# Logic attention: values ahead of the last gates and the projection between turning and right product, with four smaller edits

## The reference, cut to what matters

```
h = concat(tokens(x), txt)
h += logic_attention(ln(h))      # 8 heads: S1 = q1 k1', S2 = q2 k2', A1, A2 = softmax(S1), softmax(S2)
                                 # feat = S1, S2, S1', S2', log(A1 A2 + eps), log(A2 A1 + eps)
                                 # hid = gelu(conv1 feat), gates = sigmoid(conv2 hid)
                                 # A = softmax(mix of S1, S2, log(A1 A2) by the gates)
                                 # y = (A v1 + w A1 (A2 v2)) proj_w
h += expert_choice(ln(h))        # 8 experts take their top 28 of 113 tokens of an image, gelu MLP 128-256-128
h += relative_attention(ln(h))   # 8 heads, relative positions for keys and values
h += lstm_experts(ln(h))         # top 2 of 8 experts a token; each expert is an LSTM over the 32 images
                                 # out = h_t Wo + bo, weighted
```

## Time and profile before

| | us |
|---|---|
| median of 3 runs (2335.65 to 2337.36) | 2337.19 |
| the profiled execution's own time | 2334.96 |
| its span | 2333.2 |
| TensorE busy | 2127.5 (91%) |
| VectorE busy | 1746.5 (75%) |
| ScalarE busy | 1670.2 (72%) |
| GpSimd busy | 360.5 (15%) |
| GELU, L792, 480 of them | 451.0 |
| LSTM gates, L1871 and L1879 | 467.4 and 447.5 |
| convolution, L606 | 305.3 |

### The profile page before, as it was taken

How to read it: one execution, slowest core, us unless ns; L and a number is a source line. 1 busy time by engine, 2 the same in 40 slices (tenths; PEclk the granted TensorE clock), 3 DMA queues, 4 the chain that set the end, 5 groups by cost and what they waited for, 6 DMA issues and landing times. The chain is left out here.

```text
span 2333.2 us, 55453 instructions
## 1 busy us (share of the span) xinstructions
PE 2127.5 (91%) x22214; PEld 1521.6 (65%) x22214; DVE 1746.5 (75%) x2674; ACT 1670.2 (72%) x3076; POOL 360.5 (15%) x198
## 2 busy tenths in 40 slices
PE   6589999999999999998649799987899999999998
PEld 3454455554455554453237588856799999999997
DVE  4348999999999999998644344535788888888886
ACT  3468898888888888888723336732777777777776
POOL 0222322333322333222000013410000000000000
PEclk9589999999999999999759868998899999999999
DMA  6188888888888888888210000001222222212220
GB/s 184 57 235 236 224 228 238 233 241 239 227 224 237 232 237 239 229 228 217 61 46 1 10 2 2 1 25 74 84 77 70 72 67 77 77 61 73 71 77 21
DMA packets 113208, 305.19 MB, mean 131 GB/s; under 512 B 20495, under 2 KB 57481, under 8 KB 112442
## 3 DMA queue, kind: packets, MB, share of 16 engines
q1 hardware_dynamic: 112954, 301.66, 45.8%
HBM read 168.64 MB, written 80.65 MB: 107 GB/s over the span
## 5 line engine op out<-in xcount | busy, mean ns | idle before, releaser
L792 ACT ACTIVATE la_hid<-ps,la_b 128x904 f32<-128x904 f32 (+1 forms) x480 | 451.0, 991 | 57.3 <-PE ps L606 56.6
L1871 PE MATMUL ps<-ls_xm,ls_w_in_parts 128*128 128x226 f16 x3072 | 467.4, 261 | 4.9 <-ACT ls_cells L1921 4.3
L1879 PE MATMUL ps<-ls_state_parts,ls_w_rec_parts 128*128 128x226 f16 x2976 | 447.5, 259 | 0.0
L1921 ACT ACTIVATE ls_gates<-ps,ls_bias 128x226 f32<-128x226 f32 x768 | 301.2, 446 | 120.9 <-PE ps L1879 120.1
L606 PE MATMUL ps<-la_pairs,la_w 32*64 32x452 f32 x3584 | 305.3, 568 | 5.1 <-ACT la_hid L792 4.9
L1871 PEld LDWEIGHTS ps<-ls_xm,ls_w_in_parts 128*128 128x128 f16 x3072 | 294.2, 97 | 14.6 <-issue 3.6
L1879 PEld LDWEIGHTS ps<-ls_state_parts,ls_w_rec_parts 128*128 128x128 f16 x2976 | 284.9, 96 | 6.0
L621 PE MATMUL ps<-la_hid,la_w 128*32 128x452 f32 x1856 | 240.9, 556 | 22.4 <-ACT la_opened L798 22.4
L567 POOL TENSOR_TENSOR weights_or_rows<-la_S,la_top 113x904 f32<-113x904 f32 x64 | 133.3, 2084 | 554.3 <-DVE la_top L939 554.3
L621 PEld LDWEIGHTS ps<-la_hid,la_w 128*32 128x32 f32 x1856 | 42.3, 108 | 202.1 <-issue 94.1
L2006 DVE TENSOR_TENSOR ls_state<-ls_gates,ls_tc 128x452 f32<-128x452 f32 x128 | 80.5, 629 | 109.5 <-ACT ls_tc L1928 109.2
(11 more groups left out here) (294 smaller groups left out, 4132.1 us busy)
## 6 DMA issues: line engine op xcount, KB each, us to landing
la_pairs<-la_maps SPq DMA_DIRECT2D x224, 452.0 KB, 6.2
la_gate<-la_opened SPq DMA_DIRECT2D x448, 113.0 KB, 4.0
...
```

Of the source, the lines that this page charges most:

```text
L792: act.activation(hid[:, u % 4, 0:n], ps[:, bank:bank + n, 0:HALF], ACT.Gelu_apprx_tanh, bias=b1[:])\
L1871: mm = pe.matmul(out_j, w_in_parts[:, w, e, j, :], xm[:, t % 2, e, :, x, 0:N], start=((w, x) == PASSES[0]), stop=(t == 0 and (w, x) == PAS ...
L1879: mm = pe.matmul(out_j, w_rec_parts[:, w, e, j, :], state_parts[:, x, e], start=False, stop=((w, x) == PASSES[-1]))
L1921: return act.activation(dst, ps[:, n % 3 * 2 + j // 2, j % 2 * 256:j % 2 * 256 + C], ACT.Tanh if j == 3 else ACT.Sigmoid, bias=bias[:, e, ...
```

## The change

Five edits.

1. Logic attention, each period. TensorE runs `values(f)` before gates 7 rather than behind the turning, and `project(p + 4)` between turning and right product rather than behind `base`. VectorE copies the values first, and the projection's results directly behind the turned softmaxes. `turn_mix` waits for this period's keys (`qk_ready`).
2. Its start. The scores of images 0 to 2 go to four pairs of banks; GpSimd scales before it shifts, VectorE sums before it copies.
3. Its end. The order of the eight row groups becomes `TURNS`, groups 2 and 3 are gated and group 6 is turned earlier, the square root's table is loaded ahead, and VectorE scales the last four images.
4. Expert choice. The memset of `hid` goes to GpSimd, the wait for weights behind the gathers, and the choice of the second half of the images behind the first half's gathers.
5. LSTM experts. The bias product takes f16 in three stacked parts (48 rows: high, low, high against high, high, low), one pass; the weights are stored as two f16 parts as well.

```diff
@@ -477,9 +477,14 @@
-        def scored():
-
-            return ps[0:N, X:X + 2, 0:HALF].rearrange("p k (s m) -> p k s m", s=4)
+        def bank_of(z, i):
+
+            return (X, CB, CA, GA)[i] if z < 3 else X
+
+        def scored(z, i):
+
+            bank = bank_of(z, i)
+            return ps[0:N, bank:bank + 2, 0:HALF].rearrange("p k (s m) -> p k s m", s=4)
@@ -570,13 +575,15 @@
                     m, c, f, z = p - 1, p, p + 2, p + 3
-                    if ok(z):
+                    if ok(z) and p >= 0:
                         shift(z, 0)
...
                             pool.tensor_tensor(x, x, per_head(inv[:, i * H:(i + 1) * H]), ALU.mult).then_inc(s["P_ready"], 1)
+                    if ok(z) and p < 0:
+                        shift(z, 0)
                     if ok(z):
@@ -630,6 +637,10 @@
                             after(pe, s["added"], z - 5)
+                            after(pe, s["ST_out"], 2 * z)
+                        elif z < 3:
+                            if i == 3:
+                                after(pe, s["ych_ready"], z - 1)
                         elif i < 3:
@@ -641,19 +652,23 @@
                             sides = k[rows, col(t)], q[rows, i % 2, col(t)]
-                            mm = pe.matmul(ps[0:N, X + bank, col(2 * t + part)], *(sides if i < 2 else sides[::-1]),
+                            mm = pe.matmul(ps[0:N, bank_of(z, i) + bank, col(2 * t + part)], *(sides if i < 2 else sides[::-1]),
                                            start=True, stop=True)
...
                     after(pe, s["ln_ready"], 2 * f)
+                    if f < 2:
+                        pe.wait_ge(s["ST_out"] if i == 0 else s["S_out"], 2 * f + (4 if i == 0 else 3))
                     for hd in range(H):
...
                     pe.wait_ge(s["S_out"], 2 * min(f + 2, B))
+                    if f < 2:
+                        pe.wait_ge(s["ST_out"], 2 * f + 4)
                     pe.matmul(ps[0:N, X, 0:2 * D], hT[:, f, :], w_v[:], start=True, stop=True).then_inc(s["V_made"], 1)
@@ -679,7 +694,7 @@
                     after(pe, s["opened_ready"], PAIRS * min(e + 3, B))
-                    after(pe, s["qk_ready"], min(e + 6, B))
+                    after(pe, s["qk_ready"], min(e + 7, B))
                     after(pe, s["ych_ready"], min(e + 4, B))
@@ -705,7 +720,9 @@
                 def project(b):
-                    after(pe, s["ET_ready"], b - 5)
+                    if 0 < b < 4:
+                        pe.wait_ge(s["S_out"], 2 * b)
+                    after(pe, s["ET_ready"], b - 6)
                     after(pe, s["opened_ready"], PAIRS * min(b - 3, B))
@@ -718,7 +735,7 @@
-                    pe.wait_ge(s["rows_ready"], k + 1)
+                    pe.wait_ge(s["rows_ready"], TURNS.index(k) + 1)
                     if k == 0:
@@ -751,12 +768,16 @@
                                 score(p + 3, i, part)
+                    if ok(f):
+                        values(f)
                     if ok(p):
...
                         turn_softmax(f, 1)
-                        values(f)
+                    if ok(p + 4):
+                        project(p + 4)
+                    if ok(f):
                         right_product(f)
@@ -765,18 +786,22 @@
                                 gate_rows(four - 2)
+                        gate_rows(2)
+                        gate_rows(3)
+                    if p == B + 1:
+                        turn_rows(6)
                     if ok(f):
...
                         base(e)
-                    if ok(p + 4):
-                        project(p + 4)
                     if ok(e):
                         output(e)
-                for four in range(4, 8):
-                    turn_rows(four)
-                    gate_rows(four - 2)
+                turn_rows(4)
+                turn_rows(5)
                 gate_rows(6)
+                gate_rows(4)
+                turn_rows(7)
+                gate_rows(5)
                 gate_rows(7)
@@ -895,12 +920,13 @@
                         root(0, slice(0, EARLY))
-                for k in range(4, 7):
+                for k in (6, 4, 5):
                     scale_rows(k)
-                for k in range(4, 7):
-                    move_rows(k)
+                move_rows(6)
+                act.preload_act_table_set("sqrt_and_others")
+                move_rows(4)
                 root(1, slice(EARLY, B))
-                scale_rows(7)
+                move_rows(5)
                 move_rows(7)
@@ -1076,13 +1102,15 @@
                         mix_sum(m)
+                    if ok(f) and p < 0:
+                        sums(f)
                     if ok(z):
...
                         top_of(z, 0)
-                    if ok(f):
+                    if ok(f) and p >= 0:
                         sums(f)
@@ -1095,8 +1123,10 @@
                     if ok(f):
+                        values(f)
                         turned_softmax(f)
-                        values(f)
+                    if ok(p + 4):
+                        projected(p + 4)
                     if ok(m):
@@ -1105,13 +1135,15 @@
                         attended(e)
-                    if ok(p + 4):
-                        projected(p + 4)
                     if ok(e):
...
                 row_scale(1, slice(EARLY, B))
+                dve.wait_ge(s["row_scale"], 2)
+                for b in range(EARLY, B):
+                    x = dve.tensor_scalar(rows[:, b, :], h[:, b, :], ln["rstd"][:, b:b + 1], ln["offset"][:, b:b + 1], ALU.mult, ALU.add)
+                x.then_inc(s["rows_ready"], 1)
@@ -1207,23 +1239,26 @@
-                pe.wait_ge(consts_in, 80)
                 pe.wait_ge(s["gate_ready"], 1)
...
                 tr.then_inc(s["rows_made"], 1)
-                for k in range(2):
+                def turn_back(k):
                     pe.wait_ge(s["chosen"], k + 1)
                     pe.transpose(ps[0:N, 6 + k, 0:128], rank[:, k, :], ident[:]).then_inc(s["turned_back"], 1)
-                pe.wait_ge(s["place_ready"], 2)
+
+                turn_back(0)
                 for q in range(GROUPS):
...
                     turn(q)
+                pe.wait_ge(consts_in, 80)
                 for n in range(2 * E):
...
                         second(n - 1)
+                    if n == 1:
+                        turn_back(1)
                     if n % 2 and n < E:
@@ -1257,6 +1292,10 @@
                         take_chosen(GROUPS + n // 2)
+
+            @block.gpsimd
+            def _(pool):
+                pool.memset(hid[:], 0.0).then_inc(s["hid_zero"], 1)
@@ -1291,7 +1330,6 @@
                 steps.done(dve.memset(ones[:], 1.0))
-                dve.memset(hid[:], 0.0).then_inc(s["hid_zero"], 1)
                 scores, by_bank = scores_of(ps), peak[:].rearrange("p (k i) -> p k i", i=4)
@@ -1319,14 +1357,23 @@
                     dve.tensor_tensor(rank[:, k, :], rank[:, k, :], above[:, k, :], ALU.mult).then_inc(s["chosen"], 1)
-                for k in range(2):
+
+                def places(k):
                     dve.wait_ge(s["turned_back"], k + 1)
...
                                                 ps[0:N, 6 + k, 0:128].rearrange("p (b e) -> p b e", e=E)), s["place_ready"], k + 1)
+
+                choose(0)
+                places(0)
+                dve.wait_ge(consts_in, 80)
                 one_hot(0)
                 for q in range(GROUPS):
-                    one_hot(q + 1)
+                    if q + 1 < GROUPS:
+                        one_hot(q + 1)
                     take_back(q)
+                choose(1)
+                places(1)
+                one_hot(GROUPS)
                 for n in range(E):
@@ -1709,6 +1756,7 @@
     w_dram = nc.dram_tensor("ls_weights", (T * E * K, N), F32, kind="Internal").ap()
+    parts_dram = nc.dram_tensor("ls_weight_parts", (2, T * E * K, N), F16, kind="Internal").ap()
     halves = (slice(0, N - 1), slice(N - 1, N))
@@ -1776,6 +1828,9 @@
                     sp.dma_start(w_dram[rows, :].rearrange("(k p) n -> p k n", p=128), turned_w[:, ks, :]).then_inc(s["w_stored"], 16)
+                    for i in range(2):
+                        sp.dma_start(parts_dram[i, rows, :].rearrange("(k p) n -> p k n", p=128), turned_w_parts[:, i, ks, :])\
+                          .then_inc(s["w_stored"], 16)
@@ -1789,13 +1844,14 @@
                     rows = slice(t * E * K, (t + 1) * E * K)
-                    sp.wait_ge(s["w_stored"], 16 if t < FIRST else 32)
+                    sp.wait_ge(s["w_stored"], 48 if t < FIRST else 96)
                     if t >= 2:
...
                                  w_dram[rows, :].rearrange("r n -> (r n)").partition_broadcast(D)).then_inc(weights_in[k], 16)
-                    sp.dma_start(w_row[:, k], w_dram[rows, :]).then_inc(weights_in[k], 16)
+                    for i in range(3):
+                        sp.dma_start(w_row[E * K * i:E * K * (i + 1), k], parts_dram[i % 2, rows, :]).then_inc(weights_in[k], 16)
@@ -1826,7 +1882,7 @@
```

(26 more changed lines are left out.)

35 lines of the change are left out of this document (20 added, 15 removed).

## The result

The changed kernel takes 2346.22 us, the median of 6 runs (2340.94 to 2349.82); before takes 2337.28 in as many. The ratio is 1.0037 with a 95% interval of 1.002 to 1.0054: a little slower, with the whole interval above 1. A second set of 10 runs on another occasion gave 2341.28 and 1.002 (1.0007 to 1.0034). The forecast was 2332, inside a range up to 2342.

What follows compares the result with a forecast made beforehand. ScalarE was taken to pace part of logic attention, with no slack at L1012/L834, and TensorE the LSTM phase. Terms +22.6 - 11.7 - 6.5 - 7.1 - 7.9 + 6.0 = -4.6 gave 2332 us, range 2325 to 2339.

Steps and rivals of the forecast that it cites:

- 1. The steady period: Logic attention's repeated period: moving values and projection earlier costs +0.80 us a period, +22.6 in all (12.9 to 33).
- both routes: Steady period: delays through TensorE and through VectorE each give +0.80 us, run side by side and do not add.
- rival E: Steady period: the mix's turning waits for the projection's key copy, +1.2 us a period, 2343 us; chance 0.08.
- 2. The start: Logic attention's start: four bank pairs and scaling before shifting bring the first convolution from 143.75 to 132.0, -11.7 us.
- 3. The end: Logic attention's end: closing TensorE's idle gap and moving gate passes and one turning earlier gives -6.5 us.
- 4. Expert choice: Expert choice: memset moved, weight wait removed and half the choice deferred give -7.1 us net.
- 5. The bias product: LSTM experts: one f16 pass for two f32 passes saves 0.255 us a step, -7.9 over 31 steps.
- 6. The LSTM's start: LSTM experts' start: the masks' load, queued behind stores waiting for VectorE, comes late, +6.0 us (+3 to +6.8).
- A: Steady period: it does not grow, as filled holes on TensorE might pay; 2310 us, chance 0.12.
- B: Steady period: only the values' 0.43 us counts, +12.9 instead of +22.6; 2323 us, chance 0.13.
- D: Starts of logic attention and expert choice: the clock stays at the lower level, +3.2 and +3.4; 2339 us, chance 0.12.
- C: LSTM experts' start: the late masks' load is absorbed, since nothing ending last waits for step 1; 2326 us, chance 0.10.

Runs made afterwards that it cites:

- left product first: The four edits plus Masks first, with the left product ahead of the mix's turning and the chain copy ahead of ET's copy: 2343.13 us, ratio 1.0016.
- values alone: The changed kernel with the projection back in its old place on TensorE and VectorE: 2331.51 us, period 32.31.
- the kernel with the idle bank: The changed kernel, both moves kept, with the projection writing to the last bank, free at that time: 2329.85 us, period 32.50.
- the projection alone: The changed kernel with the values back behind the turning on TensorE and behind the turned softmaxes on VectorE: 2332.52 us, period 32.72.
- the four edits: The changed kernel with both moves of the steady period (values and projection) undone: 2307.38 us, ratio 0.9847.
- Masks first: The four edits, with SyncE issuing the load of step 1's masks directly behind the masks' store: 2306.74 us, ratio 0.9871.
- padded: Masks first, with the output bias product's operands padded by rows of zeros from 48 to 128: 2300.43 us, ratio 0.9833.
- queue in order: The padded kernel, with masks' load, f32 weights' store and broadcast loads issued ahead of the f16 parts, on separate semaphores: 2297.27 us, ratio 0.9836.
- the old start: The queue in order kernel with logic attention's start as before (one bank pair, GpSimd shifts before scaling): 2309.17 us, ratio 0.9866.

## Why the prediction was wrong, point by point

**What bounded the kernel.** Right in kind, not in full. I read L1012 and L834 as a pair without slack. The chain copy alone was last; ScalarE had 0.14 to spare (left product first, and values alone: 0.76 at the opening gave 0.61).

**1. The steady period: the step that failed.** Summed: +0.80 a period, +22.6. Measured: +1.17 a period, 30 to 32 us. With the wait of the mix's turning taken away the period is 31.70 + 0.80, so the total of the sum held. In part that is luck. In the kernel with the idle bank the turning of the softmaxes was 0.76 late where I had 0.43; from there to the right product it took 2.57 (476.66 to 479.23) for 2.44 before (513.89 to 516.33), 0.13 more where I had 0.37; and the turning of the mix followed 1.59 behind the right product for 1.68. That is 0.76 + 0.13 - 0.09 = 0.80 again. What failed is the line that both routes run side by side. The change ties them together: L685 waits for VectorE's last copy of the projection. That is rival E, with a chance of 0.08 and 2343, and it is what happened; I had its deciding point wrong. I wrote that the wait decides when the copy ends after 519.1. But by my own sum TensorE would reach the turning of the mix at 518.01 + 0.80 = 518.81, and at this wait TensorE started 0.26 behind the end of the copy (519.68 to 519.94): the point was 518.55, and I had the copy at 518.7, past it already. The 0.26 could not be read from before. There the right product, at 516.33, starts 0.05 behind the end of the copy it waits for:

```profile
515.20 1.08 DVE L988 COPY la_PT<-ps 113x904 f32<-113x904 f32 x1
```

With 0.05 the point would have been 518.76, and my copy 0.06 short of it, not 0.4. Why this wait takes 0.26 no run shows. The copy ended, counted on before's scale, at 518.86, a further 0.16 late, because the turning came 0.76 late and not 0.43. With the projection alone, where the turning is not late, it ended at 518.70 on that scale (480.90, with the opening at 476.20), and the period still grew by 1.02.
The values' 0.43 was the second mis-sized term: 0.76 at the opening, since I took one pass' tail off a duration in a place where the product breaks a run of another shape. Alone that gives 0.61 a period; beside the other move it hardly shows, as the chain copy ends last by more.
The last two periods grew too (32.3 and 30.5 to 32.2, for 31.7 and 30.1), which I had at 0.43 and 0.

**2. The start.** Summed -11.7; measured -8.5 and -11.6 up to the fifth logarithm in the changed kernel, -16.6 with the four edits, 11.9 by the medians of its own experiment. The number held in one of the two profiles, and by luck, for the way was another: the first convolution came at 122.45 and 125.24, not 132.0, with the clock up from about 100, and 13 and 7 us of the gain were given back in the next periods, in which ScalarE waits for a store and the granted clock falls, which the walk-through ended too early to see. The two moves take at most the 5 to 8 between the table's columns.

**3. The end.** Summed -6.5, measured -7.0 and -7.4, and -6.9 with the four edits alone. Right. Masks first, padded, queue in order and the old start, with the same end, lie between -7.3 and -4.7.

**4. Expert choice.** Summed -7.1, measured -7.8 in both profiles, up to relative attention: one_hot begins 15.4 after the last gate pass, for 25.2 before, and the late half gives 2 of that back. Right.

**5. The bias product.** Summed -7.9 (at best -10.5, at worst -6.2), measured -6.4. The pass went away and neither way in nor way out shrank: what the rule of the Trainium skill on draining gave (6.2), not the half way that I took. That the changes of tile are what kept them long is shown by the padded product.

**6. The LSTM's start.** Summed +6.0, measured +6.8 and +7.0, where the end that I gave was 6.8. The stores took 2.3 instead of 1.3, and from issue to use the load took 5.20 instead of 4.49. The estimate from the Trainium skill's figure, a stall 1.4 shorter, was further off; the trace was the better source. In "Anatomy of one DMA" that figure is fitted to transfers that GpSimd issues, and this load is issued by SyncE, which I had passed over.

**The sum.** The terms for the four edits came to -27.2; they measure 27 by the spans of the profiles, 30 by the medians and 36 by the ratio. The time lies 9 to 14 above the forecast, and the spans of the two profiles 19 and 11 above the sum on before's 2333.2. The largest part is the steady period's term, 9 and 8. Relative attention, code that nothing in the change touches, is another 6 and 3, the start 3 and 0, the bias 1.5 and the LSTM's start 1; the end and expert choice gave 1 back. Rivals A, B and D are out: the period grew, by more than the values, the start's clock rose early, and expert choice gave its whole term. C is out: the late load was not absorbed. E is what happened.

What stays open: how much of the start's loss is the DMA queue and how much the clock. Both move together in each profile, and no run here parts them. Open too is why relative attention's granted clock differs from one profile to the next.
